# The mixer's last stores are waited for in the dense weights stage

## The chip, the core and the metric

The program runs on one core of one Trainium2 chip, whose five engines (PE for matmuls, DVE, ACT, POOL, and SP, which here only issues transfers) each run their own instruction stream. The metric is the device time of one execution in microseconds, lower is better.

## The reference, cut to what matters

```python
h = tok(log_dt, Lambda, x, 1024)            # (64, 128, 1024), from exponentials of position
h = concatenate([h, txt], axis=1)           # (64, 205, 1024)
h = h + attn(layernorm(h), A_log, D, x_proj_w, dt_proj_w, dt_proj_b)
h = h + ffn(layernorm(h), qweight, lut4, lut8, bias)

# tok:  Wc = W * (exp(dt*Lam) - 1) * reciprocal((exp(dt*Lam*L) - 1) * Lam)
#       K = einsum('chn,hnl->chl', Wc, exp(dt*Lam * pos)).real
# attn: a state recurrence over the 205 rows, 1024 channels x 16 states
#       h = dA_t * h + dBx_t;  y_t = einsum('bdn,bn->bd', h, C_t);  y + D * x
# ffn:  idx = the 4-bit (or 8-bit) code of each weight, unpacked from bit planes
#       w = take_along_axis(lut, idx);  y = einsum('bsi,oi->bso', x, w) + bias
#       rows whose norm is over 64 take the 8-bit weights, the others the 4-bit ones
```

## The kernel before

The program is a row of stages. Each stage is one block (`nc.Block()`): a piece of code for each engine, and at the end of the block all five engines meet before any of them starts the next one. The stages are, in order:

- `constants`: small tables, and the loads of `qw` (the packed weight codes) and `lut`.
- `token_mixer`, up to 299.6 us: `tok` for all 64 batches. It goes through 128 heads in 16 groups of eight. For a group, DVE and ACT make sines and exponentials, POOL joins them, PE multiplies (L438), and ACT copies the products from PSUM into `t_res`, which has two halves, one for even groups and one for odd (L286). SP stores a half to `mixed` in DRAM with two transfers of 512 KB (L257), each adding 16 to the half's count `out_done`. ACT waits on that count before it writes a half again.
- `dense_weights`, 311.3 to 479.6 us: it builds the feed-forward weights `w_low` from `qw` and `lut`. DVE takes the bits apart (L471 to L475, L543), ACT casts the codes (L579), DVE makes a mask for each of 16 codes (L554), POOL makes scaled diagonals (L570), PE adds them up in 192 matmuls for each of eight output blocks (L603), ACT and DVE copy the sum (L588, L558), and PE turns it with 32 narrow matmuls (L614). It reads nothing of the mixer's, and SP has no work in it.
- `scan_pass`, to the end but for some 10 us: the recurrence and the feed-forward part, batch by batch. SP loads rows of `mixed` at its start (L805).
- `general_path`: only its test of a flag runs here.

The mixer's last lines on SP (L267 to L270) store the last two groups and then wait until both counts are full. `t_res` and the counts belong to the mixer's own context and are free for other use from its end on. The Python contexts in `build` (L1511 on) say which buffers live through which stages: `early` holds `qw` and `lut` through the mixer and the dense stage, and is closed ahead of the scan.

Of the kernel before, what the change touches and what calls it, by code (L numbers as in the profile page):

```python
# [13 lines left out]
F32 = mybir.dt.float32  # L14
# [6 lines left out]
P = 128  # L21
# [9 lines left out]
QL = LK // NQ  # L31
# [8 lines left out]
HG = 8  # L40
NG = HEADS // HG
# [7 lines left out]
def wait(engine, sem, value):  # L49

    if isinstance(value, int) and value <= 0:
        return
    engine.wait_ge(sem, value)
# [118 lines left out]
def token_mixer(nc, t, dram, mixed):  # L172
# [5 lines left out]
    with ExitStack() as ctx:  # L178
        sb = lambda n, s, d=F32: ctx.enter_context(nc.sbuf_tensor(n, s, d))
        sem = lambda n: ctx.enter_context(nc.semaphore(n))  # L180
# [25 lines left out]
        near = sb("t_near", [P, HG // 2 * QL])  # L206
        mag = sb("t_mag", [P, 2, HG * QL])
        osc = sb("t_osc", [P, HG * QL])
        res = sb("t_res", [P, 2, HG, 2, QL])

        turns_ps = ctx.enter_context(nc.psum_tensor("t_turns_ps", [P, HG // 2 * QL], F32))
        turned_x = ctx.enter_context(nc.psum_tensor("t_turned_x", [P, 2, 512], F32))
# [7 lines left out]
        mag_done, sine_done, table = sem("t_mag_done"), sem("t_sine_done"), sem("t_table")  # L220
        full = [sem(f"t_full{i}") for i in range(4)]
        empty = [sem(f"t_empty{i}") for i in range(4)]
        out_done = [sem(f"t_out_done{i}") for i in range(2)]
        block = ctx.enter_context(nc.Block())

        def loop(engine, step, tail=None):
# [13 lines left out]
        @block.sync  # L240
        def _(sp):
            sp.dma_start(ldt[:, :], dram["log_dt"].rearrange("h r -> (h r)").unsqueeze(0).broadcast_to([P, 2 * HEADS])).then_inc(loaded, 16)
            for k in range(2):
                sp.dma_start(lam[64 * k:64 * k + 64, :], dram["Lambda"]).then_inc(loaded, 16)

            def load(G, half):

                wait(sp, x_turned, G - 1)
                for side in range(2):
                    sp.dma_start(xg[64 * side:64 * side + 64, half, :].rearrange("c (h m) -> c h m", h=HG // 2),  # L250
                                 x[:, bass.ds(G * HG + HG // 2 * side, HG // 2), :]).then_inc(x_in[half], 16)

            def store(G, half):
                for b in range(4):
                    wait(sp, empty[b], 2 * G + 2)
                for a in range(2):
                    sp.dma_start(mixed[:, bass.ds(G * HG, HG), :].rearrange("c h (b a l) -> a c h b l", b=2, a=2)[a],  # L257
                                 res[64 * a:64 * a + 64, half, :, :, :]).then_inc(out_done[half], 16)

            load(0, 0)  # L260
            load(1, 1)
            with sp.Fori(1, NG // 2) as i:
                load(i * 2, 0)
                store(i * 2 - 2, 0)
                load(i * 2 + 1, 1)
                store(i * 2 - 1, 1)
            store(NG - 2, 0)  # L267
            store(NG - 1, 1)
            for half in range(2):
                sp.wait_ge(out_done[half], 32 * (NG // 2))  # L270

        @block.scalar
        def _(act):
# [220 lines left out]
def dense_weights(nc, t, dram):  # L494
# [3 lines left out]
    with ExitStack() as ctx:  # L498
        sb = lambda n, s, d=F32: ctx.enter_context(nc.sbuf_tensor(n, s, d))
        sem = lambda n: ctx.enter_context(nc.semaphore(n))  # L500
# [17 lines left out]
        turned, stored_0, stored_1 = sem("q_turned"), sem("q_stored_0"), sem("q_stored_1")  # L518
        block = ctx.enter_context(nc.Block())
        PAIRS = CODES // 2  # L520

        def target(o, half):
            return t["w_low"][:, 4 * half:4 * half + 4, o * P:o * P + P]

        @block.vector
        def _(dve):
# [19 lines left out]
            def store(o):  # L546
                wait(dve, turned, o + 1)
                V.tensor_scalar(target(o, 1), t_ps[1][:, :].rearrange("p (i c) -> p i c", i=4), 1.0, None, ALU.mult).then_inc(stored_1, 1)

            for o in range(ND):  # L550
                dve.wait_ge(cast, o + 1)
                for c in range(CODES):
                    wait(dve, used, (o * CODES + c - MASKS) // 2 + 1)
                    V.tensor_scalar(mask[:, c % MASKS, :], codes[:, o * DIM:o * DIM + DIM], float(c), None, ALU.is_equal).then_inc(mask_done, 1)  # L554
                    if o and c == 3:
                        store(o - 1)
                wait(dve, used, o * PAIRS + PAIRS)
                V.tensor_scalar(w_rows[:, 1, :], w_ps[:, 1, :], 1.0, None, ALU.mult).then_inc(copied_1, 1)  # L558
# [3 lines left out]
        def _(pool):  # L562
            pool.wait_ge(prepared, 1)
            each = CODES // 2 * 3
            for o in range(ND):
                for side in range(2):

                    wait(pool, used, (o - 1) * PAIRS + (side + 1) * PAIRS // 2)
                    first = o * CODES * 3 + side * each
# [6 lines left out]
        def _(act):  # L576
# [9 lines left out]
            for o in range(ND):  # L586
                wait(act, used, o * PAIRS + PAIRS)
                nc.scalar.activation(w_rows[:, 0, :], w_ps[:, 0, :], ACT.Copy).then_inc(copied_0, 1)  # L588
# [3 lines left out]
        def _(pe):  # L592
            for o in range(ND):
                for pair in range(PAIRS):
                    pe.wait_ge(diagonal_done, o * 2 + pair // (PAIRS // 2) + 1)
                    pe.wait_ge(mask_done, o * CODES + 2 * pair + 2)
                    for k in range(3):
                        for half in range(2):
                            for odd in range(2):
                                c = 2 * pair + odd  # L600
                                for i in range(2):
                                    q = slice(64 * i, 64 * i + 64)
                                    last = nc.tensor.matmul(  # L603
                                        w_ps[64 * odd:64 * odd + 64, i, 512 * half:512 * half + 512],
                                        diagonal[q, c // PAIRS, c % PAIRS * 3 + k, :], mask[q, c % MASKS, 512 * half:512 * half + 512],
                                        start=(pair == 0 and k == 0), stop=(pair == PAIRS - 1 and k == 2))
# [597 lines left out]
def general_path(nc, t, dram, kept, before, out):  # L1204

    any_over(nc, t)
    with ExitStack() as ctx:
        general_weights(nc, t, dram, kept, t["flag"], ctx)
        general_rows(nc, t, t["flag"], before, out)
# [283 lines left out]
def persistent(nc, ctx):  # L1498

    t = {}  # L1500
    for name, shape, dtype in (
            ("ident", [P, P], F32), ("sel8", [P, 8], F32), ("code_col", [P, 1], F32),
           
            ("a_neg", [P, ND, NS], F32), ("d_col", [P, ND], F32), ("xp_one", [XP, 1], F32), ("y_bias", [P, ND], F32),
            ("xpw_t", [P, ND, XP], F32), ("dtw_t", [RANK + 1, DIM], F32), ("ln_in", [P, 2, 2, 2], F32),
            ("ve_all", [P, BATCH, 2], F32), ("minus_half", [P, 2], F32), ("eps_ln", [P, 1], F32), ("flag", [1, 1], I32)):
        t[name] = ctx.enter_context(nc.sbuf_tensor(name, shape, dtype))
    return t


def build(nc, dram, out):  # L1511
    mixed = nc.dram_tensor("mixed", (BATCH, HEADS, LK), F32, kind="Internal").ap()
    before = nc.dram_tensor("before", (BATCH, LEN, DIM), F32, kind="Internal").ap()
    rows_bc = nc.dram_tensor("rows_bc", (2, 2 * NS, LEN), F32, kind="Internal").ap()
    kept = {"spread": nc.dram_tensor("spread_kept", (P, 16 * P), BF16, kind="Internal").ap()}
    with ExitStack() as ctx:
        t = persistent(nc, ctx)
        with ExitStack() as low:
            t["w_low"] = low.enter_context(nc.sbuf_tensor("w_low", [P, ND, DIM], F32))
            with ExitStack() as early:  # L1520
                t["qw"] = early.enter_context(nc.sbuf_tensor("qw", [P, 4, ND, 32], I32))
                t["lut"] = early.enter_context(nc.sbuf_tensor("lut", [P, ND * CODES], F32))
                with ExitStack() as first:
                    t["ramp"] = first.enter_context(nc.sbuf_tensor("ramp", [P, HALF], F32))
                    constants(nc, t, dram, kept)
                    token_mixer(nc, t, dram, mixed)
                dense_weights(nc, t, dram)
            scan_pass(nc, t, dram, mixed, before, rows_bc, out)
        general_path(nc, t, dram, kept, before, out)
# [24 lines left out]
```

## Time and profile before

| | |
|---|---|
| median of three runs | 6210.84 us (6210.68 to 6211.06) |
| profiled execution, its own time | 6212.96 us |
| its span | 6211.1 us |
| mean granted clock of PE | 0.978 of full speed |
| busy share: PE, DVE, ACT, POOL | 93%, 92%, 82%, 92% |
| from the mixer's last issue to the dense stage's first instruction | 299.62 to 311.25 us |
| dense weights stage | 311.25 to 479.55 us |
| first ring product of the scan | 515.87 us |

Times in the rows are from the start of the span. A row of the timeline gives the start, the time from the first to the last of the merged instructions, the engine, the line, the operation with what it writes and reads, and in brackets how long the engine had been idle and what ended that. PEclk in a window is the clock that was granted to PE: 1.00 is the high level, 2.4 GHz, and 0.50 the low one, 1.2 GHz.

### The profile page before, as it was taken

How to read it: one execution, taken by the hardware profiler on the slowest of the kernel's cores; microseconds unless marked ns; L12 is line 12 of the kernel's file. 1: busy time of each engine (PE TensorE's matmuls, PEld its weight loads, DVE VectorE, ACT ScalarE, POOL GpSimd, SP SyncE). 2: the span in 40 equal slices, each digit the busy share in tenths (PEclk: the TensorE clock that was granted, in tenths of full speed). 3: DMA queues.
4: the chain of work that ended last, by engine and by line, in shares of the span. 5: the costliest groups of instructions: out<-in, count | busy, mean ns of one | idle time of the engine just before them, and what ended most of it. 6: DMA issues, size and time to landing. Idle time of an engine off the chain costs nothing. (4 is left out here: it accounts for less than half of the span.)

```text
span 6211.1 us, 111922 instructions
## 1 busy us (share of the span) xinstructions
PE 5793.1 (93%) x35091; PEld 5384.9 (87%) x35091; DVE 5698.9 (92%) x4564; ACT 5123.3 (82%) x12831; POOL 5709.9 (92%) x3484
## 2 busy tenths in 40 slices
PE   4676999999999999999999999999999999999998
PEld 3545899999999999999999999999999999999997
DVE  8776999999999999999999999999999999999996
ACT  5716888888888888888888888888888888888884
POOL 4526999999999999999999999999999999999995
PEclk9887999999999999999999999999999999999999
DMA  4701221222122211222122212221222112221220
GB/s 94 160 2 66 83 82 61 77 88 87 60 77 86 88 71 68 83 88 77 61 83 88 82 62 77 88 83 61 77 88 88 68 71 83 88 77 61 83 82 34
DMA packets 115881, 478.49 MB, mean 77 GB/s; under 512 B 17441, under 2 KB 52401, under 8 KB 107122
## 3 DMA queue, kind: packets, MB, share of 16 engines
q1 hardware_dynamic: 115314, 471.10, 22.0%
q8 instruction: 335, 5.49, 0.4%
q14 instruction: 232, 1.90, 0.1%
HBM read 327.82 MB, written 143.24 MB: 76 GB/s over the span
## 5 line engine op out<-in xcount | busy, mean ns | idle before, releaser
L1103 POOL TENSOR_TENSOR s_ring<-s_bc,s_u_t 128x820 f32<-128x820 f32 x2048 | 3618.3, 1788 | 4.4 <-DMA s_bc<-rows_bc 4.4
L999 ACT ACTIVATE s_decay<-s_dt_t,a_neg 128x205 f32<-128x205 f32 x8192 | 3047.3, 420 | 418.4 <-DVE s_ring L1164 346.7
L895 PE MATMUL s_y_ps<-s_ring,ident 128*128 128x205 f32 x16384 | 3140.5, 341 | 115.3 <-issue 61.6
L895 PEld LDWEIGHTS s_y_ps<-s_ring,ident 128*128 128x128 f32 x16384 | 2863.3, 191 | 207.4 <-POOL s_ring L1109 115.4
L1158 DVE TENSOR_TENSOR_SCAN s_decay<-s_decay,s_ring 128x820 f32<-128x820 f32 x1216 | 2265.0, 1863 | 192.9 <-ACT s_decay L999 178.9
L1109 POOL TENSOR_TENSOR s_ring<-s_ring,s_bc 128x820 f32<-128x820 f32 x832 | 1605.3, 1929 | 78.3 <-DVE s_ring L1158 78.2
L1158 DVE TENSOR_TENSOR_SCAN s_ring<-s_decay,s_ring 128x820 f32<-128x820 f32 x832 | 1542.8, 1854 | 41.9 <-ACT s_decay L999 41.1
L928 PE MATMUL s_xch<-s_x_t,w_low 128*128 128x205 f32 x8192 | 1524.3, 338 | 0.5 <-ACT s_x_t L1042 0.2
L928 PEld LDWEIGHTS s_xch<-s_x_t,w_low 128*128 128x128 f32 x8192 | 1422.6, 190 | 35.3 <-issue 30.5
L1164 DVE TENSOR_TENSOR s_ring<-s_decay,s_bc 128x820 f32<-128x820 f32 x1216 | 1229.5, 1011 | 41.8
L889 PE MATMUL s_y_ps<-s_x_t,s_d_diag 128*128 128x205 f32 x1024 | 279.1, 354 | 35.2 <-ACT s_x_t L1037 35.2
L1042 ACT ACTIVATE s_x_t<-s_xch 128x512 f32<-128x512 f32 (+1 forms) x512 | 244.6, 503 | 67.3 <-PE s_xch L919 65.7
L1124 POOL TENSOR_TENSOR s_u_t<-s_dt_t,s_x_t 128x410 f32<-128x410 f32 x256 | 271.8, 1062 | 18.2 <-DVE s_dt_t L1186 18.2
L1056 ACT ACTIVATE s_y_t<-s_xch,y_bias 128x205 f32<-128x205 f32 x512 | 213.6, 417 | 90.0 <-PE s_xch L928 89.9
L1037 ACT ACTIVATE s_x_t<-s_y_ps 128x205 f32<-128x205 f32 x512 | 169.8, 332 | 139.4 <-PE s_y_ps L895 138.6
L960 PE MATMUL s_p_ps<-s_xp,dtw_t 33*128 33x205 f32 x1024 | 248.1, 363 | 7.6 <-DVE s_dt_t L1186 7.1
L438 PE MATMUL t_kb<-t_mag,t_gw 128*128 128x256 f32 x512 | 139.6, 432 | 104.9 <-POOL t_gw L320 104.9
L889 PEld LDWEIGHTS s_y_ps<-s_x_t,s_d_diag 128*128 128x128 f32 x1024 | 169.4, 189 | 75.9 <-ACT s_x_t L1037 58.0
L960 PEld LDWEIGHTS s_p_ps<-s_xp,dtw_t 33*128 33x128 f32 x1024 | 166.2, 188 | 66.5 <-issue 56.9
L438 PEld LDWEIGHTS t_kb<-t_mag,t_gw 128*128 128x128 f32 x512 | 107.1, 216 | 127.8 <-POOL t_gw L320 62.6
L1193 DVE TENSOR_TENSOR s_h<-s_xch,s_h 128x512 f32<-128x512 f32 (+1 forms) x256 | 172.6, 675 | 38.9 <-PE s_xch L942 38.9
L951 PE MATMUL s_p_ps<-s_x_t,xpw_t 128*65 128x205 f32 x1024 | 200.9, 339 | 0.6 <-ACT s_x_t L1042 0.6
(165 smaller groups left out, 4223.5 us busy)
## 6 DMA issues: line engine op xcount, KB each, us to landing
s_bc<-rows_bc SPq DMA_DIRECT2D x64, 3280.0 KB, 11.0
mixed<-t_res SPq DMA_DIRECT2D x32, 1024.0 KB, 9.6
s_x_in<-mixed SPq DMA_DIRECT2D x64, 512.0 KB
s_h<-mixed SPq DMA_DIRECT2D x64, 512.0 KB
before<-s_h SPq DMA_DIRECT2D x64, 512.0 KB
out<-s_h SPq DMA_DIRECT2D x64, 512.0 KB
s_x_in<-in_txt SPq DMA_DIRECT2D x64, 308.0 KB
s_h<-in_txt SPq DMA_DIRECT2D x64, 308.0 KB
```

The lines of the kernel that those rows point to most:

```text
L438: last = nc.tensor.matmul(kb[b][:, QL * k:QL * k + QL], gw[:, half, h, 2 * k:2 * k + 2, :], mag[:, half, h * QL:(h + 1) * QL], start=True, ...
L889: nc.tensor.matmul(y_ps, d_diag[:, j, :], x_t[:, par, j, :], start=True, stop=False)
L895: last = nc.tensor.matmul(y_ps, ident[:, :], ring[:, c % RING, n * LEN:(n + 1) * LEN], start=False, stop=(c % 4 == 3 and n == CN - 1))
L928: last = nc.tensor.matmul(bank[:, 0:LEN], t["w_low"][:, i, P * o:P * o + P], x2_t[:, i, :], start=(i == 0), stop=(i == ND - 1))
L960: last = nc.tensor.matmul(p_ps[:, LEN * k:LEN * k + LEN], t["dtw_t"][:, P * j:P * j + P], xp[0:RANK + 1, :], start=True, stop=True)
L999: last = A.activation(decay[s % 2][:, n * LEN:(n + 1) * LEN], dt_t[:, par, j, :], ACT.Exp, scale=t["a_neg"][:, j, n0 + n:n0 + n + 1])
L1042: A.activation(target[:, 4 * side:4 * side + 4, cols(k)], bank[:, 0:4 * w].rearrange("p (j l) -> p j l", j=4), ACT.Copy).then_inc(empty, 1)
L1103: nc.gpsimd.tensor_tensor(ring[:, s % RING, :].rearrange("p (n l) -> p n l", n=CN), bc[:, par, n0:n0 + CN, :], u_t[:, j, :].unsqueeze(1).b ...
L1109: nc.gpsimd.tensor_tensor(ring[:, c % RING, :], ring[:, c % RING, :], bc[:, par, n0:n0 + CN, :].rearrange("p n l -> p (n l)"), ALU.mult).t ...
L1124: nc.gpsimd.tensor_tensor(u_t[:, 2 * r:2 * r + 2, :], dt_t[:, par, 2 * r:2 * r + 2, :], x_t[:, par, 2 * r:2 * r + 2, :], ALU.mult).then_in ...
L1158: V.tensor_tensor_scan(out=decay[s % 2] if s in ON_DVE else ring[:, s % RING, :], data0=decay[s % 2], data1=ring[:, s % RING, :], initial= ...
L1164: V.tensor_tensor(ring[:, s % RING, :], decay[s % 2], bc[:, par, n0:n0 + CN, :].rearrange("p n l -> p (n l)"), ALU.mult).then_inc(dve_hc, 1)
```

## The change

`t_res` and the two `out_done` counts are made in `early` rather than in the mixer, so that they live until the dense stage is over. The two waits move from the end of the mixer's block on SP to a new SP part of the dense stage's block. No other line differs; below the new lines the line numbers shift by up to 7.

```diff
 def token_mixer(nc, t, dram, mixed):
-        res = sb("t_res", [P, 2, HG, 2, QL])
+        res = t["res"]
...
-        out_done = [sem(f"t_out_done{i}") for i in range(2)]
+        out_done = t["out_done"]
...
             store(NG - 2, 0)
             store(NG - 1, 1)
-            for half in range(2):
-                sp.wait_ge(out_done[half], 32 * (NG // 2))
...
 def dense_weights(nc, t, dram):
...
+        @block.sync
+        def _(sp):
+            for half in range(2):
+                sp.wait_ge(t["out_done"][half], 32 * (NG // 2))
...
 def build(nc, dram, out):
...
             with ExitStack() as early:
                 t["qw"] = early.enter_context(nc.sbuf_tensor("qw", [P, 4, ND, 32], I32))
                 t["lut"] = early.enter_context(nc.sbuf_tensor("lut", [P, ND * CODES], F32))
+                t["res"] = early.enter_context(nc.sbuf_tensor("t_res", [P, 2, HG, 2, QL], F32))
+                t["out_done"] = [early.enter_context(nc.semaphore(f"t_out_done{i}")) for i in range(2)]
```

SP is the only engine whose instructions change. Before, at the end of the mixer and the start of the scan, its stream reads as follows; a wait in brackets is made ahead of the instruction, the first branch leaves the mixer's block, and the second enters the scan's after the meeting of all engines.

```order
L257 DMA mixed<-t_res 64x16x256 [waits t_empty2,t_empty3,t_empty1,t_empty0]
L257 DMA mixed<-t_res 64x16x256
L178 UNCONDITIONAL_BRANCH [waits t_out_done1,t_out_done0]
L802 UNCONDITIONAL_BRANCH [waits barrier_Pool_Activation_PE_DVE_SP_release]
L805 DMA s_x_in<-mixed 128x1024
L806 DMA s_x_in<-in_txt 77x1024
```

The same place now, where the first branch leaves the mixer's block, the second enters the dense stage's and the third leaves it:

```order
L257 DMA mixed<-t_res 64x16x256 [waits t_empty2,t_empty3,t_empty1,t_empty0]
L257 DMA mixed<-t_res 64x16x256
L178 UNCONDITIONAL_BRANCH
L521 UNCONDITIONAL_BRANCH [waits barrier_Pool_Activation_PE_DVE_SP_release]
L497 UNCONDITIONAL_BRANCH [waits t_out_done1,t_out_done0]
L806 UNCONDITIONAL_BRANCH [waits barrier_Pool_Activation_PE_DVE_SP_release]
L809 DMA s_x_in<-mixed 128x1024
L810 DMA s_x_in<-in_txt 77x1024
```

The waits on the two counts stand behind one meeting of the engines instead of ahead of it, and there are two more branches.

## Rows read from the trace of the kernel before

**Rows 1.** SP's waits, 290 to 520 us: engine, line, waited for, us, times, longest.

```profile
SPq L498 <- PEq L498: 168.5, 1, 168.5
...
SPq L270 <- DMA mixed<-t_res: 11.1, 1, 11.1
```

**Rows 2.** Timeline of all engines, 296 to 345 us: start, us, engine, instruction, idle before.

```profile
297.63 0.60 ACT L286 ACTIVATE t_res<-t_kb 128x512 f32<-128x512 f32 x1 [0.27 <-PE t_kb L438]
298.31 1.31 SPq L257 DMA_DIRECT2D mixed<-t_res  x2
311.25 0.41 DVE L531 COPY q_stack<-ident 64x64 f32<-64x64 f32 x2 [28.64 <-PEq L178]
...
314.46 5.61 POOL L570 TENSOR_TENSOR q_diagonal<-q_stack_bf,q_lut_part 128x1536 bf16<-128x1536 bf16 x2 [22.40 <-DVE q_part L539]
...
337.18 7.68 ACT L579 ACTIVATE q_codes<-q_wide 128x1024 bf16<-128x1024 int32 x8 [38.95 <-DVE q_wide L543]
```

**Rows 3.** Windows: busy us by engine, then PEclk, DMA share, GB/s.

```profile
302.00:306.00 4.00, 0.00 (x0) 0.00 (x0) 0.00 (x0) 0.00 (x0) 0.00 (x0) 0.50 0.91 206
310.00:311.00 1.00, 0.00 (x0) 0.00 (x0) 0.00 (x0) 0.00 (x0) 0.00 (x0) 0.50 0.15 48
```

**Rows 4.** Timeline of PE and ACT in the dense weights stage, 339 to 480 us.

```profile
339.18 13.22 PE L603 MATMUL q_w_ps<-q_mask,q_diagonal 64*64 64x512 bf16 x192 [41.59 <-DVE q_mask L554]
...
353.82 3.76 PE L614 MATMUL q_t_ps<-q_stack,q_w_rows 128*128 128x64 f32 x32 [1.42 <-DVE q_w_rows L558]
357.51 10.55 PE L603 MATMUL q_w_ps<-q_mask,q_diagonal 64*64 64x512 bf16 x192
...
368.12 1.02 ACT L588 ACTIVATE q_w_rows<-q_w_ps 128x1024 f32<-128x1024 f32 x1 [9.90 <-PE q_w_ps L603]
...
369.44 4.79 PE L614 MATMUL q_t_ps<-q_stack,q_w_rows 128*128 128x64 f32 x32 [1.38 <-ACT q_w_rows L588]
374.16 12.80 PE L603 MATMUL q_w_ps<-q_mask,q_diagonal 64*64 64x512 bf16 x192
...
387.02 1.02 ACT L588 ACTIVATE q_w_rows<-q_w_ps 128x1024 f32<-128x1024 f32 x1 [12.16 <-PE q_w_ps L603]
...
471.66 1.02 ACT L588 ACTIVATE q_w_rows<-q_w_ps 128x1024 f32<-128x1024 f32 x1 [9.90 <-PE q_w_ps L603]
...
472.99 5.84 PE L614 MATMUL q_t_ps<-q_stack,q_w_rows 128*128 128x64 f32 x32 [1.38 <-ACT q_w_rows L588]
```

**Rows 5.** Windows in which the granted clock changed level.

```profile
344.00:345.00 1.00, 1.00 (x20) 0.51 (x16) 0.44 (x2) 0.86 (x1) 0.00 (x0) 0.68 0.00 0
371.00:372.00 1.00, 1.00 (x11) 1.00 (x10) 1.00 (x4) 0.00 (x0) 0.00 (x0) 0.97 0.00 0
378.00:379.00 1.00, 1.00 (x16) 0.48 (x12) 0.00 (x0) 0.00 (x0) 0.00 (x0) 0.62 0.00 0
474.00:475.00 1.00, 1.00 (x9) 1.00 (x8) 0.00 (x0) 0.00 (x0) 0.00 (x0) 0.67 0.00 0
501.00:502.00 1.00, 1.00 (x6) 0.71 (x5) 0.00 (x0) 0.00 (x0) 0.00 (x0) 0.68 0.11 37
```

**Rows 6.** Timeline around the scan's start.

```profile
478.86 0.69 DVE L548 TENSOR_SCALAR w_low<-q_t_ps 128x512 f32<-128x512 f32 x1 [5.98 <-PE q_t_ps L614]
479.83 0.10 POOL L1138 MEMSET s_large<- 128x4 f32 x1 [20.99 <-POOLq L498]
...
497.48 5.01 PE L951 MATMUL s_p_ps<-s_x_t,xpw_t 128*65 128x205 f32 x16 [0.61 <-ACT s_x_t L1042]
...
504.55 0.34 SPq L838 DMA_DIRECT2D s_bc<-rows_bc  x1
...
515.87 5.24 POOL L1103 TENSOR_TENSOR s_ring<-s_bc,s_u_t 128x820 f32<-128x820 f32 x3 [4.36 <-DMA s_bc<-rows_bc]
```

**Rows 7.** POOL's longest wait in the scan.

```profile
POOL s_ring L1109 <- DVE s_ring L1158: 78.2, 124, 2.1
```

**Rows 8.** A window inside the scan.

```profile
1000.00:2000.00 1000.00, 973.54 (x5649) 916.77 (x5648) 949.89 (x718) 869.00 (x2215) 980.30 (x603) 0.99 0.22 80
```

## The prediction

> **What bounds the kernel now.** I first read the busy shares of the page: PE, DVE and POOL are all over 90% busy, which is an average over stages with different limits and says nothing about the place of the change. So the second view was the windows by stage. From about 516 us to the end the scan runs with POOL 98% busy [rows 8], and its longest wait there is 78.2 us in 124 pieces, for DVE [rows 7]; that stage takes some 5,690 of the 6,211 us and the change touches no instruction of it. What the change can move lies before it, between the mixer's last store and the first instruction of the dense weights stage.
>
> The third view was SP's own waits [rows 1]. SP waits once for the landing of the mixer's stores, at L270, for 11.1 us, and after that for 168.5 us for the other engines to finish the dense weights stage, in which it has no work. The fourth was the timeline of that place [rows 2]. ACT's last copy into t_res starts at 297.63 and ends at 298.23; SP issues the two last stores from 298.31 to 299.62; then nothing runs on any engine until DVE begins the dense stage at 311.25. DVE had been idle 28.64 us, POOL 22.40 us, and PE 41.59 us by the time of its first matmul at 339.18 [rows 2, 4]. In 302 to 306 us the DMA engines are 91% busy and every compute engine at 0.00; in 310 to 311 the DMA is down to 15% [rows 3]. So 299.62 + 11.1 = 310.7 is where the last store has landed, and 0.5 us more passes until DVE starts. All five engines stand still for a transfer that the next stage doesn't read: the dense stage works on qw and lut, and mixed is read first by the scan's load at 479.83 and later.
>
> **The change part by part.** The wait leaves the mixer's block. SP then reaches the block's end at 299.62 rather than 310.7. It was the last to arrive: ACT was done at 298.23, PE, DVE and POOL earlier. With the same 0.5 us for the meeting of the engines, DVE starts at 300.15. Gain: 11.1 us, all of it on the path, for from DVE's first instruction the stage is one chain: DVE's words and masks, ACT's cast at 337.18, then PE from 339.18 until the last copies at 478.86 [rows 2, 4, 6].
>
> The wait comes back as SP's only work in the dense block. It ends at about 310.7, and that block ends at about 468 on the slowest engine, so it costs nothing; nothing is queued behind it on SP but the scan's first load, which waits for the end of the block anyway. The cover is 157 us; if it were gone the cost would be the old 11.1 us. SP passes two more branches, beside the other engines' branches at the same places. The boundary between the dense stage and the scan, which has such branches and no DMA wait, takes from 479.55 (DVE's last copy ends) to 479.83 [rows 6], 0.28 us, so I put the extra ones at 0, between 0 and 0.3 us.
>
> t_res (32 KB a partition) and two counts now live through the dense stage. That only moves addresses; no instruction gets another shape. I cost it at 0; from the trace no gain or loss can be read, and the bound is the 0.5 us of the boundary either way.
>
> The two stores' traffic now runs beside DVE's and POOL's first 11 us. Those read and write SBUF only and wait for no DMA. In the scan POOL stays 98% busy beside a mean of 80 GB/s [rows 8], so I cost this at 0, with at most 0.5 us of loss.
>
> Next the clock of PE, which is what makes the rest of the stage uncertain. After its long idle time PE runs at the low level (0.50 granted, 1.2 of 2.4 GHz) from 339.18 to about 344.7 [rows 5], and the first 192 matmuls take 13.22 us, where 192 at the high level take 10.55 [rows 4]: 5.5 us at the low level cost 2.67 us. From then on the clock falls again in four places after the narrow L614 matmuls that follow an output block: the first fall is just before 372 and the last at 474.3, each of the first three lasts about 6.8 us (372 to 378.6) [rows 5]. Their price: ACT's reading of a block comes 18.90 us after the one before it where a fall lies between (368.12 to 387.02). The six periods from 368.12 to 471.66 take 103.54 us; three have a fall, so the others take (103.54 - 3 x 18.90) / 3 = 15.61. A fall costs 3.29 us. The last lengthens the last L614 group from 3.76 to 5.84, 2.08 us [rows 4].
>
> Whether and when it falls in the shifted stage the trace of before can't show. For the start, the low stretch can be anything from none (2.67 us gained) to longer than now; the nearest row of another start is the scan's, where matmuls begin at 497.48 and the clock rises at about 501.7, 4.2 us later [rows 5, 6]. With 4.2 in place of 5.5 us, the gain is 1.3 x 2.67 / 5.5 = 0.6 us. I take 0.6. For the falls: as many as now is 0, one fewer -3.3, one more +3.3. I take 0 for the forecast and keep both ends.
>
> The Trainium skill (TensorE: Matmul & The Clock Gate, Part 1) says that the unit that watches PE is free-running and doesn't restart with a kernel, so that the moment of a change depends on where the first matmul falls. By that rule a shift of 11.1 us re-deals the falls; by a rule in which the clock followed PE's own work alone, the stage would be repeated exactly and the sum would be -11.1. The rows here fit the first: equal blocks follow each other, and only every second one has a fall.
>
> On the scan's start: its first ring product on POOL waits for the s_bc load, issued at 504.55 behind the L951 matmuls of 5.01 us, which run mostly at the low level [rows 6]. Another moment of the rise moves this by at most 0.7 us either way; I take 0. The scan itself, bound by POOL, I take as unchanged.
>
> Sum: -11.1 - 0.6 = -11.7 us. The profiled execution took 6212.96 us with a span of 6211.1; it becomes 6201.3. The median of the runs shown is 6210.84, 2.1 us below the profiled one, so the time is 6210.84 - 11.7 = 6199.1. I state 6199.0.
>
> **The rivals.** A: one fall of the clock fewer. For it: the stage has eight places where it can fall and four where it does, the last at its very end; a shift may leave that one or another out. Against it: nothing in before says so. Time: 6199.1 - 3.3 = 6195.8, with the start of the stage unimproved 6196.4.
>
> B: one fall more. For it the same openness; against it that after a fall the next block never has one. Time: 6202.4.
>
> C, slower than before: a fall after every output block instead of every second. It would sit at the eight L614 groups, seven whole ones and the last: 7 x 3.29 + 2.08 = 25.1 us, against 3 x 3.29 + 2.08 = 12.0 now, so 13.1 us lost against 11.1 gained: +2.0, 6212.8. It turns to the slower side from four more falls on (4 x 3.29 = 13.2). Were PE kept at the low level for the whole stage, it would be far slower. Against it: four blocks in eight keep the high level with the same idle gap of 1.4 us before L614.
>
> D, the stall stays in another form: the engines jump to the dense stage's code while the stores fill the DMA engines, and the code comes late. At the most DVE waits until 310.7 as now: no gain, 6210.8. Against it: DVE idles from 282.6 on, long before the jump, and in the scan every engine jumps back to the head of a long loop beside a mean of 80 GB/s of transfers, and POOL is 98% busy there [rows 8]. The Trainium skill (Runtime: NRT & Kernel Launch, Instruction fetch mechanics) says that a taken branch to code outside the present window forces a DMA fetch before execution goes on, which would speak against this change; the boundary at 479.55 to 479.83 shows no such stall, though it has no other traffic beside it.
>
> E, the change doesn't do what it says: something else at the end of the mixer's block waits for the stores. The order of SP's instructions has no such wait, and the other engines wait only for SP. Time 6210.8.
>
> **How the numbers follow.** The forecast (-11.7, four falls) has 0.46, with a range of its own of 6198.0 to 6200.2. A has 0.33, B 0.08, C 0.03, D and E together 0.07, and 0.03 is left for what I haven't thought of. A measurement of this kernel can tell about 0.2%, 12.4 us, from no change: the border is 6198.4, and the forecast lies only 0.7 us from it. All of A is beyond it, and about a third of the forecast's share: faster 0.33 + 0.15 = 0.48. Slower by over 0.2% needs more than C: 0.03. Same takes 0.49. The range reaches from A's lower end, 6195.2, to B's upper end, 6202.6, and leaves out D, E and C.
>
> **What would show it.** In the profile of the changed kernel SP has no wait at the mixer's end; DVE's q_stack copy starts at 300.1 to 300.4, with the DMA engines about 90% busy for the next 10 us; ACT's cast starts at about 326.1 and PE's first L603 matmul at 328.1. SP's wait for out_done shows about 10 us inside the dense stage. The first 192 matmuls take about 12.6 us. The scan's first load is issued near 468.1, and from there to the end the length is that of before within 1.5 us. If DVE starts at 311 again, D or E is right. If the dense stage is 3 us shorter or longer from PE's first matmul to its last, the windows must show one fall of the granted clock fewer or more. If the gain at 300 us is there and gone by the end with the same falls, then the scan takes back what it is given, and my reading of it as independent is wrong.

## The result and the profile after

The changed kernel takes 6200.56 us (median of 22 runs, 6192.81 to 6205.34) against 6210.76 us before (22 runs, 6206.17 to 6219.45): 10.2 us less, a ratio of 0.9984 with a 95% interval of 0.9978 to 0.9991. So the gain is between 5.6 and 13.7 us. The prediction said 6199.0.

The profiled execution took 6200.29 us, with a span of 6198.4. SP's own waits in it, as in [rows 1]: line, waited for, us, times, longest.

```profile
SPq L497 <- PEq L497: 158.0, 1, 158.0
...
SPq L524 <- DMA mixed<-t_res: 10.4, 1, 10.4
```

What is waited for are the last two stores, of 1 MB each (`t_res` 64x16x256 in fp32; the 512 KB said in the description of the kernel before are too low by half). The wait for them is still 10.4 us, but now it lies inside the dense stage (L524), ahead of the 158.0 us in which SP waits for the others anyway. The timeline of the place, as in [rows 2]:

```profile
297.13 1.31 SPq L257 DMA_DIRECT2D mixed<-t_res  x2
...
299.13 0.41 DVE L535 COPY q_stack<-ident 64x64 f32<-64x64 f32 x2 [17.75 <-PEq L178]
...
302.34 5.62 POOL L574 TENSOR_TENSOR q_diagonal<-q_stack_bf,q_lut_part 128x1536 bf16<-128x1536 bf16 x2 [10.24 <-DVE q_part L543]
...
325.12 7.68 ACT L583 ACTIVATE q_codes<-q_wide 128x1024 bf16<-128x1024 int32 x8 [28.08 <-DVE q_wide L547]
```

SP's last issue ends at 297.13 + 1.31 = 298.44 and DVE starts 0.69 us later, where it had been 11.63 (299.62 to 311.25). Its idle time went from 28.64 to 17.75 us. That is the gain: 10.94 us. The windows, as in [rows 3, 5]; the columns are busy us of PE, PEld, DVE, ACT and POOL, then PEclk, DMA share and GB/s:

```profile
304.00:306.00 2.00, 0.00 (x0) 0.00 (x0) 1.97 (x2) 0.00 (x0) 2.00 (x2) 0.50 1.01 244
...
332.00:333.00 1.00, 1.00 (x20) 0.48 (x13) 0.50 (x2) 0.80 (x1) 0.00 (x0) 0.77 0.00 0
...
359.00:360.00 1.00, 1.00 (x10) 1.00 (x10) 1.00 (x4) 0.00 (x0) 0.00 (x0) 0.89 0.00 0
...
366.00:367.00 1.00, 1.00 (x20) 0.49 (x16) 0.00 (x0) 0.00 (x0) 0.00 (x0) 0.70 0.00 0
...
462.00:463.00 1.00, 1.00 (x8) 1.00 (x7) 0.00 (x0) 0.00 (x0) 0.00 (x0) 0.59 0.00 0
```

In the first one DVE and POOL are fully busy while the stores fill the DMA engines: the two run side by side now. DVE's first instruction to PE's first matmul took 27.93 us before and takes 27.99 now, so the traffic beside them costs nothing that can be seen. The other windows are the places where PE's clock changes level. Then PE and ACT in the dense stage, as in [rows 4]:

```profile
327.12 13.18 PE L607 MATMUL q_w_ps<-q_mask,q_diagonal 64*64 64x512 bf16 x192 [30.71 <-DVE q_mask L558]
...
345.40 10.55 PE L607 MATMUL q_w_ps<-q_mask,q_diagonal 64*64 64x512 bf16 x192
...
357.33 4.83 PE L618 MATMUL q_t_ps<-q_stack,q_w_rows 128*128 128x64 f32 x32 [1.38 <-ACT q_w_rows L592]
...
362.10 12.76 PE L607 MATMUL q_w_ps<-q_mask,q_diagonal 64*64 64x512 bf16 x192
...
460.87 5.87 PE L618 MATMUL q_t_ps<-q_stack,q_w_rows 128*128 128x64 f32 x32 [1.38 <-ACT q_w_rows L592]
```

```profile
356.00 1.02 ACT L592 ACTIVATE q_w_rows<-q_w_ps 128x1024 f32<-128x1024 f32 x1 [9.90 <-PE q_w_ps L607]
...
374.91 1.23 DVE L562 TENSOR_SCALAR q_w_rows<-q_w_ps 128x1024 f32<-128x1024 f32 x1 [1.86 <-PE q_w_ps L607]
...
459.54 1.22 DVE L562 TENSOR_SCALAR q_w_rows<-q_w_ps 128x1024 f32<-128x1024 f32 x1 [4.42 <-PE q_w_ps L607]
```

The pattern of before is there again, 12.1 us earlier: a low start (13.18 us for the first 192 matmuls, where 10.55 is the price at the high level), a fall after the second, fourth and sixth block and one at the end. The stage takes 168.33 us from DVE's first instruction to its last copy; it was 168.30. And the start of the scan, as in [rows 6], with POOL's longest wait in it, as in [rows 7]:

```profile
467.74 0.10 POOL L1142 MEMSET s_large<- 128x4 f32 x1 [21.02 <-POOLq L497]
...
485.44 4.95 PE L955 MATMUL s_p_ps<-s_x_t,xpw_t 128*65 128x205 f32 x16 [0.61 <-ACT s_x_t L1046]
...
503.63 6.98 POOL L1107 TENSOR_TENSOR s_ring<-s_bc,s_u_t 128x820 f32<-128x820 f32 x4 [4.21 <-DMA s_bc<-rows_bc]
```

```profile
POOL s_ring L1113 <- DVE s_ring L1162: 77.6, 124, 2.1
```

From the scan's first instruction to its first ring product it is 35.89 us (36.04 before), and from there to the flag at the end 5686.1 (5686.9). The 12.7 us between the two spans are, in order: 1.18 in the mixer, whose last issue ends at 298.44 and not at 299.62; 10.94 at the boundary; none in the dense stage; 0.15 and 0.83 in the scan; and 0.37 given back behind the flag. Only the 10.94 lie where the change was made, and the median gain of 10.2 us agrees with them.

### The profile page after: what moved, and what is told of

Same layout as the page of the kernel before. It is cut to its first block and busy times, and to the rows that moved or that the text cites. A ratio compares the mean times of both kernels' runs of the same rounds, so it can differ in the third digit from the quotient of the medians.

```text
span 6198.4 us, 111922 instructions
## 1 busy us (share of the span) xinstructions
PE 5792.6 (93%) x35091; PEld 5385.1 (87%) x35091; DVE 5699.7 (92%) x4564; ACT 5122.6 (83%) x12831; POOL 5709.3 (92%) x3484
```

## The experiments

Where a kernel was timed, it was on the same chip as runs of the kernel before; that kernel's median was 6213.69 us beside the first four and 6208.18 beside the second four. The first four ran on one chip, the second four on another, so an expected time that started from 6210.8 us is read as a difference to the kernel before of its set. Traces differ by a few microseconds in the scan, so what a trace shows and what the medians show are told apart below.

**e1_wait_back.** The new place of t_res, the old place of the wait:

```diff
 # after.py, mixer's block on SP
             store(NG - 2, 0)
             store(NG - 1, 1)
+            for half in range(2):
+                sp.wait_ge(out_done[half], 32 * (NG // 2))
 # dense stage: its block.sync part is taken out
```

> The changed kernel with the two waits put back at the end of the mixer's block; t_res and the counts still live through the dense stage. Theory (the wait alone is what stood in the way, where the buffer lies costs nothing): DVE's q_stack copy starts near 311 again, 11.6 us after SP's last issue, and the time is that of before, 6210.8, within 3 us. Rival (the new placement or the longer life of t_res brings part of the gain): the time stays 3 to 10 us under 6210.8 although the wait is there. Rival that the placement costs something: over 6214.

Measured: 6214.22 us against 6213.69, ratio 1.0004 (0.9994 to 1.0013). The timeline at the boundary:

```profile
296.77 1.31 SPq L257 DMA_DIRECT2D mixed<-t_res  x2
...
309.62 0.41 DVE L532 COPY q_stack<-ident 64x64 f32<-64x64 f32 x2 [28.59 <-PEq L178]
```

The gap from SP's last issue (298.08) to DVE is 11.54 us again, and SP's wait is 11.0 us. The gain at the boundary is gone with the wait alone. The time is 0.5 us above the kernel before of its set, between 3.7 below and 8.1 above by the interval; 6214.22 is over the 6214 of the second rival, but the kernel before of this set takes 6213.69 itself. The theory holds. The first rival, 3 to 10 us under, is left only its last 0.7 us by the interval; the second, a cost of over 3 us, isn't excluded by the time, but the trace shows no such cost: the dense stage takes 165.87 us, which is what e0 below has with the same three falls of the clock.

**e2_more_stores.** The kernel before with the suspected cost doubled:

```diff
 # before.py
+    spill = nc.dram_tensor("spill", (BATCH, HG, LK), F32, kind="Internal").ap()
...
             store(NG - 1, 1)
+            for a in range(2):
+                sp.dma_start(spill[:, :, :].rearrange("c h (b a l) -> a c h b l", b=2, a=2)[a],
+                             res[64 * a:64 * a + 64, 1, :, :, :]).then_inc(out_done[1], 16)
             for half in range(2):
-                sp.wait_ge(out_done[half], 32 * (NG // 2))
+                sp.wait_ge(out_done[half], 32 * (NG // 2 + half))
```

> The kernel before with two further transfers of 1 MB each from t_res to a scratch tensor behind the mixer's last stores, counted in the same wait: the suspected cost doubled. Theory (all five engines stand still until the last byte lands, and the stall goes into the time one for one): the 2 MB take 11.1 us now, 4 MB some 21 to 22, so SP's wait at the end of the mixer grows by 9.5 to 11 us and the time goes from 6210.8 to about 6221 (6218 to 6224). Rival (the time from the stall is partly given back by the later stages): the wait grows as much, but the time by less than 6 us.

Measured: ratio 1.0018 (1.0009 to 1.0028), 6225.17 us against 6213.69, so 11.5 us more (5.6 to 17.4 by the interval). The boundary:

```profile
298.06 1.31 SPq L258 DMA_DIRECT2D mixed<-t_res  x2
...
299.42 8.16 SPq L271 DMA_DIRECT2D spill<-t_res  x2
...
320.82 0.41 DVE L535 COPY q_stack<-ident 64x64 f32<-64x64 f32 x2 [38.51 <-PEq L179]
```

From the end of the last mixed store (299.37) to DVE's start it is 21.45 us, 9.8 more than before, in spite of the 8.16 us that SP spends on issuing the two extra transfers: it is the landing that counts. SP's wait itself is 12.7 us, only 1.6 more, since the issuing of the extra transfers takes the place of most of it; the theory's 9.5 to 11 us hold for the stall and not for the wait. The stall goes into the time about one for one. The interval is too wide to tell 9.8 from 11.5; of the rival's range, less than 6 us, it leaves in the last 0.4.

**e3_gap_filled.** PE works through the gap behind each output block, into a bank that nothing reads:

```diff
 # after.py, dense stage, PE; spare is a new [128, 512] PSUM tensor
+                for _ in range(5):
+                    nc.tensor.matmul(spare[0:64, :], stack_bf[:, :], codes[:, 0:512], start=True, stop=True)
                 pe.wait_ge(copied_0, o + 1)
                 pe.wait_ge(copied_1, o + 1)
```

> The changed kernel with five bf16 matmuls of 512 columns into a spare PSUM bank put behind the 192 matmuls of each output block in the dense stage, where PE waits about 1.4 us for the copies. Their results are not used. Theory (the falls of PE's clock in this stage come from the idle gap and the narrow matmuls behind it falling together, and cost 3.29 us each and 2.08 at the last): the falls after the output blocks go away, the dense stage gets shorter by up to 12 us, and the time is 6189 to 6194, with less scatter from run to run than the 6193 to 6205 of the changed kernel. Rival (the narrow L618 matmuls alone are too little for the high clock): as many falls as now, time 6200 to 6202, the same scatter.

The five matmuls, the turn and the next block in it:

```profile
340.56 1.27 PE L614 MATMUL q_spare<-q_codes,q_stack_bf 128*64 128x512 bf16 x5
...
342.06 3.76 PE L621 MATMUL q_t_ps<-q_stack,q_w_rows 128*128 128x64 f32 x32 [0.22 <-DVE q_w_rows L563]
...
345.74 10.55 PE L608 MATMUL q_w_ps<-q_mask,q_diagonal 64*64 64x512 bf16 x192
```

And one window over most of the stage, first of the changed kernel, then of this one:

```profile
340.00:450.00 110.00, 100.29 (x1404) 64.59 (x1400) 75.11 (x116) 11.35 (x14) 37.22 (x13) 0.91 0.01 2
```

```profile
340.00:450.00 110.00, 108.69 (x1616) 67.75 (x1609) 78.83 (x126) 11.35 (x14) 37.22 (x13) 1.00 0.01 2
```

The granted clock is 1.00 in this window and not 0.91. The five take 1.27 us of the 1.4 us gap, every L621 group 3.76 us and every block 10.55, and the dense stage takes 156.37 us rather than 168.33: 11.96 us shorter, where 3 x 3.29 + 2.08 = 11.95 had been worked out from the falls. The narrow matmuls alone do not bring the clock down; behind the idle gap they do. Whether the gap would do it without narrow matmuls behind it was not tried. The prediction's prices for the four falls were right in their sum, and the rival is out. Of the other traces so far, before, after, e2 and e4 have four falls and e1 has three, all with the gap open; e5 and e8 below have the gap filled and none, so this isn't a matter of one execution.

The time fell less clearly: 6196.72 us, ratio 0.9973 (0.9963 to 0.9983), 17.0 us under before, where 10.9 + 12 = 23 were to be expected; the interval, 10.6 to 23.0 us, just reaches that. The expected 6189 to 6194 us were missed. The scan of this trace takes 5690.0 us from the ring's first product to the flag, 3.9 more than in the trace of the changed kernel; but that was taken beside another set of runs, and the scans of all four traces of this set are long (5689.0 to 5694.1). The scatter, 6193.5 to 6200.3 in nine runs, is less than the changed kernel's 12.5 us in 22, as was said, but more than the expected range.

**e4_warm_start.** PE works ahead of the first block:

```diff
 # after.py, dense stage, PE, ahead of the loop over output blocks
+            pe.wait_ge(wide_done, 1)
+            for _ in range(30):
+                nc.tensor.matmul(spare[0:64, 0:384], stack_bf[:, :],
+                                 lut_part[:, :, :].rearrange("p c k -> p (c k)"), start=True, stop=True)
```

> The changed kernel with 30 bf16 matmuls of 384 columns into a spare PSUM bank at the start of the dense stage, while DVE still makes the code words, so that PE works for some 7 us before its first useful matmul. Their results are not used. Theory (the first 192 matmuls take 13.2 us rather than 10.55 only because of the low clock at the start): they take 10.6 us, and the time falls by 2.7 us to about 6198, the falls after the output blocks being as many as now. Rival (the low start only re-deals the later falls): the first 192 get faster, but the stage has one fall more or fewer, so the time is 6194.5 or 6201.

```profile
319.08 7.32 PE L600 MATMUL q_spare<-q_lut_part,q_stack_bf 128*64 128x384 bf16 x30 [21.95 <-DVE q_wide L548]
...
327.96 10.55 PE L611 MATMUL q_w_ps<-q_mask,q_diagonal 64*64 64x512 bf16 x192 [1.56 <-DVE q_mask L559]
```

The first 192 matmuls take 10.55 us instead of 13.18, so the cost of the low start, 2.6 us, is what the prediction read from two rows. The falls are four as before, and the stage takes 165.93 us, 2.4 less. In the time it doesn't show: 6202.42 us where about 6198 was expected, ratio 0.9983 (0.9974 to 0.9992), the same as the changed kernel's 0.9984. 2.6 us is 0.04%, less than half the width of the interval. The profiled run was among the longest of its eleven (6207.4 us), with 5693.9 us in the scan.

**e0_after_again.** The changed kernel, without an edit, beside the next three.

> The changed kernel itself, run again beside the other kernels of this set. Theory (the gain is the one stall of 10.9 to 11.1 us, and what differs from run to run comes from the scan, whose length from the first ring product to the flag was 5686.1 to 5694.1 us in six traces while the dense stage kept its length to 0.1 us): median 10 to 12 us below that of before, the dense stage 168.3 us long again if it has four falls of the clock and 165.9 if it has three. Rival (the gain itself depends on the run): a median less than 8 or more than 14 us below before.

Measured: 6196.44 us against 6208.18, ratio 0.9983 (0.9974 to 0.9992), 11.7 us as medians. Its trace has a boundary of 0.69 us again and only three falls of the clock in the dense stage, at 359, 393 and 427 us, none at the end:

```profile
426.16 5.80 PE L618 MATMUL q_t_ps<-q_stack,q_w_rows 128*128 128x64 f32 x32 [1.38 <-ACT q_w_rows L592]
...
445.03 3.76 PE L618 MATMUL q_t_ps<-q_stack,q_w_rows 128*128 128x64 f32 x32 [1.38 <-ACT q_w_rows L592]
...
460.65 3.76 PE L618 MATMUL q_t_ps<-q_stack,q_w_rows 128*128 128x64 f32 x32 [1.38 <-ACT q_w_rows L592]
```

The first 192 matmuls take 12.88 us and the stage 165.87, 2.46 less than in the other trace of this program: 0.30 of it are the start and some 2.1 the missing last fall. The same program thus has three falls in one execution and four in another. e1, whose wait stands where it did before, had three as well (165.87 us). That is what the forecast and rival A differed in, and it isn't a property of the change.

**e5_both.** The edits of e3 and e4 together.

> The changed kernel with both fillings of PE's idle time in the dense stage: 30 matmuls ahead of the first useful one and five after each output block, none of whose results are used. Theory (the two costs of the low clock are separate and add up, 2.6 and 12.0 us): the dense stage takes 168.3 - 14.5 = 153.8 us, and the time is 14 us below that of the changed kernel, 25 us below before. Rival (the scan starts later in its own terms and gives a part back, as its 4 us more in the two single fillings suggest): the dense stage is as short, but the time only 8 to 11 us below the changed kernel.

Measured: 6187.62 us, ratio 0.9967 (0.9955 to 0.9979), 20.6 us under before and 8.8 under the changed kernel as medians. In the trace the dense stage takes 153.89 us with no fall, 14.4 less than 168.33: the two costs add up. The time lies in the rival's range. Its reason isn't seen in this trace: the scan takes 5683.5 us, less than in any trace before it, and starts in 35.85. But this was the shortest of the six runs (6183.4 us, 4.2 under their median), so what the scan does in a median run is not shown, and the rival isn't out. Part of the missing gain is that e0's trace had only three falls to lose (its stage is 165.87, so there are 12.0 us to gain against it and not 14.4). The rest, some 3 us, stays open.

**e7_early_load.** SP issues the scan's first load inside the dense stage, behind its new wait:

```diff
 # after.py, dense stage, SP (s_x_in and its count are made in build, ahead of both stages)
             for half in range(2):
                 sp.wait_ge(t["out_done"][half], 32 * (NG // 2))
+            sp.dma_start(t["x_in"][:, 0, :], t["mixed"][0, :, :]).then_inc(t["x_loaded"], 16)
+            sp.dma_start(t["x_in"][0:TXT, 1, :], dram["txt"][0, :, :]).then_inc(t["x_loaded"], 16)
...
 # scan, SP
-            rows_of(x_in, 0, loaded)
```

> The changed kernel in which SP, once the stores have landed, also issues the scan's first load (rows of mixed and txt for batch 0, 0.8 MB) inside the dense stage; the buffer s_x_in is made ahead of both stages. Theory (that load's 4.7 us from issue to ACT's first use are bare at the start of the scan, as the stores' landing was at the end of the mixer, only the 1.3 us of ACT's table load remain): the first ring product comes 3.3 us sooner after the end of the dense stage, 32.6 rather than 35.9, and the time is 3 us below the changed kernel. Rival (the s_bc load or the clock of PE takes its place): the first ring product comes less than 1.5 us sooner.

The load, and the start of the scan:

```profile
310.35 0.35 SPq L525 DMA_DIRECT2D s_x_in<-mixed  x1
```

```profile
465.12 0.10 POOL L1143 MEMSET s_large<- 128x4 f32 x1 [22.18 <-POOLq L497]
...
465.25 1.28 ACT L981 ACT_TABLE_LOAD   x1 [0.50 <-POOL s_large L1143]
...
466.54 1.06 ACT L1020 ACTIVATE s_xn<-s_x_in 128x1024 f32<-128x1024 f32 x1
```

ACT's first use comes right behind its table load. From the scan's first instruction to the first ring product it is 32.52 us, where the changed kernel has 35.89 and 36.54 in its two traces: 3.4 and 4.0 us less, as the theory said, so the rival is out. In the time no gain can be seen: 6196.92 us against 6196.44 for e0, ratio 0.9980 (0.9971 to 0.9989) against 0.9983. The load's issue comes 11.1 us after the end of the last store's (299.24), so beside DVE and POOL the stores land no later than in the kernel before. This trace has three falls too, but after the third, fifth and seventh block, behind a first block of 11.86 us:

```profile
327.91 11.86 PE L609 MATMUL q_w_ps<-q_mask,q_diagonal 64*64 64x512 bf16 x192 [30.71 <-DVE q_mask L560]
...
356.81 3.76 PE L620 MATMUL q_t_ps<-q_stack,q_w_rows 128*128 128x64 f32 x32 [1.38 <-ACT q_w_rows L594]
...
372.43 4.75 PE L620 MATMUL q_t_ps<-q_stack,q_w_rows 128*128 128x64 f32 x32 [1.38 <-ACT q_w_rows L594]
```

**e8_all.** The edits of e3, e4 and e7 together.

> The changed kernel with both fillings and the early load: the version that is to beat both. Theory (three separate pieces): 14.5 + 3.3 = 17.8 us below the changed kernel, 28 to 29 below before. Rival (they take from each other or the scan gives back 4 us): 12 to 15 below the changed kernel.

Measured: 6181.48 us (6179.14 to 6182.87), ratio 0.9957 (0.9944 to 0.9971): 26.7 us under before and 15.0 under the changed kernel run beside it. It is below both medians. The dense stage takes 153.95 us and the start of the scan 32.63, so both pieces are there in full. Against e0's trace that is 165.87 - 153.95 + 36.54 - 32.63 = 15.8 us, and 15.0 were measured; the theory's 17.8 had been reckoned against a trace with four falls. The time lies at the upper end of the rival's 12 to 15 us, so by the time alone it isn't told from the theory. The trace shows nothing given back later, the scan takes 5683.0 us from the ring's first product to the flag, but it is of the shortest of five runs, 2.3 us under their median.

## Why the prediction was right

- **The stall at the boundary.** Said: 11.1 us, DVE 0.5 us behind SP's last issue. Measured: 10.94 us, 0.69 behind. e1 shows that the stall stands and goes with the wait alone, and e2 that a longer landing lengthens it. Reading the full stop of all engines in the timeline, and its ending together with the DMA's, was the step that carried the sum.
- **The wait at its new place, two more branches, t_res's longer life, the traffic beside DVE and POOL.** All costed at 0. The dense stage's length of 168.33 against 168.30 us, with four falls of the clock in both, shows it for the sum of them; e1's trace shows it for the placement.
- **The low start of PE's clock.** Said: 0.6 us gained, from the row of another start. Measured: 13.18 instead of 13.22 us, so none of it. The term was mis-sized, within its bounds. The start isn't a property of the change either: with the same PE code the first 192 matmuls take 13.18 us in one trace and 12.88 in e0, and 11.86 in e7. Its full price is 2.63 us by e4, where 2.67 had been read.
- **The falls.** Said: as many as now. The profile after has four again, and that was luck: e0 shows three for the same program. The sum of their prices was confirmed by e3, 11.96 us against 11.95. So rival A was not an alternative to the forecast: both happen, in different executions. The shape of the question was wrong where it asked what the change would do to the falls. A's price was off too: it named the last fall as the one that might be left out and took 3.3 us for it, where the prediction's own price for the last is 2.08, and e0 shows some 2.1.
- **The scan.** Said: unchanged within 1.5 us, since POOL bounds it. In the pair of before and after it was (0.98 us with its start). Over ten traces of all kernels the stretch from the first ring product to the flag is 5683.0 to 5694.1 us, so as a statement on any two traces this margin was too small by far, and that it held in the pair is in part luck. Much of the difference goes with the set, and so perhaps with the chip, which the prediction didn't think of: 5686.9 and 5686.1 in the pair, 5689.0 to 5694.1 in the four traces of the first set, 5683.0 to 5687.5 in those of the second, and the medians of the kernel before are ordered the same way (6210.76, 6213.69 and 6208.18 us). One place of it is POOL's wait for ACT's ln_in, first in e0, then in e2:

```profile
POOL s_rstd L1138 <- ACT ln_in L1036: 28.9, 21, 2.0
```

```profile
POOL s_rstd L1138 <- ACT ln_in L1036: 34.7, 23, 2.1
```

  5.8 us of the 10.0 us between these two traces' scans stand there. The longest single wait is nearly the same; what decides how often it comes was not tried. This stays open.
- **The code comes late (rival D).** DVE's 0.69 us behind SP's last issue, with the DMA engines busy, against the 0.5 us of the meeting before, leaves room for 0.2 us of it at the most. The Trainium skill's rule that a taken branch to distant code stalls (Runtime: NRT & Kernel Launch, Instruction fetch mechanics) isn't contradicted by that, but nothing of it is seen here: DVE had idled for 17.75 us.
- **C and E** are out: no trace has more than four falls, and the wait was gone.
- **The chances.** The measured gain of 10.2 us lies on the near side of the 12.4 us border, where the forecast lay with 0.7 us to spare. I had put nearly half beyond the border for a 3.3 us rival and a 0.6 us term. The interval of the gain, 5.6 to 13.7 us, reaches over the border, so the time supports the 11.1 us term and can't tell terms of this size; only the traces do. That the median came within 1.6 us of the forecast is in part good fortune.

## What to carry to other kernels

A wait for stores at the end of a stage makes every engine pay for the landing when the engines meet there; if the next stage neither reads what was stored nor needs the buffer, its place is the next stage, on the queue that has nothing to do. The gain can be read off before building: from the last issue to the first instruction behind the meeting, less the 0.7 us that the meeting itself took here. And look at what PE does in its short pauses: here two fillings of idle time with matmuls that nobody reads took 12.0 us more off the dense stage in the traces (e5 against e0) and 8.8 us off the median, where the change itself gave 10.9 us in the pair of traces and 11.7 us as medians of that set.

## What the runs showed of the hardware

PE's granted clock fell behind a pause of 1.4 us followed by 3.8 us of narrow matmuls, and didn't in any of 24 places (eight each in e3, e5 and e8) once 1.27 us of the pause were filled with five 512-column matmuls. Equal work never had a fall at two places in a row, in e7 none at the first two, and the same program had three falls in one execution and four in another, 2.5 us apart in the stage's length. The Trainium skill (TensorE: Matmul & The Clock Gate, Part 1) says that the unit which watches PE is free-running; the two traces of one program, at 168.33 and 165.87 us, agree with it.

DVE and POOL lost nothing that can be seen beside stores at 182 to 244 GB/s (2 us windows from 300 to 308 us): 27.99 us against 27.93 from DVE's first instruction of the stage to PE's first matmul.
